# Four value projections of the next pair moved from the end of a part into its middle, and two GpSimd additions tied to later events

## The reference

```
x = LN(x + attention0(x))          # 16 heads of 64, full softmax, output projection + bo
x = LN(x + routed_ffn(x))          # scores against 8 clusters and 64 tiles, two argmaxes pick one
                                   # tile a token; its small spline network scales a direction
x = LN(x + attention1(LN(x)))      # linear attention and a 65-wide window attention, gated, + x
x = LN(x + moe(LN(x)))             # causal attention with normalised q, k; then 8 experts of
                                   # 128 -> 512 -> 128, all computed, mixed by a softmax gate
```

## Time and profile before

| what | us |
|---|---|
| runs (3) | 2326.81, 2313.84, 2310.08; median 2313.84 |
| profiled execution | 2315.99, span 2314.2 |
| TensorE busy | 2190.1 (95% of the span) |
| VectorE, ScalarE, GpSimd busy | 1601.9, 1344.2, 849.3 |
| mean granted TensorE clock | 0.984 of full |

### The profile page before, as it was taken

How to read it: one execution, slowest core, us unless ns; L and a number is a source line. 1 busy time by engine, 2 the same in 40 slices (tenths; PEclk the granted TensorE clock), 3 DMA queues, 4 the chain that set the end, 5 groups by cost and what they waited for, 6 DMA issues and landing times.

```text
span 2314.2 us, 44705 instructions
## 1 busy us (share of the span) xinstructions
PE 2190.1 (95%) x16091; PEld 1532.7 (66%) x16091; DVE 1601.9 (69%) x5015; ACT 1344.2 (58%) x3784; POOL 849.3 (37%) x1010
## 2 busy tenths in 40 slices
PE   8999999999999999999999999999999999999897
PEld 6655666856668566776667666686666856667465
DVE  5666686686767867678775778758676686766752
ACT  5336574764657656576556657476564765646542
POOL 3313471055510644117521356114561064510630
PEclk9999999999999999999999999999999999998999
DMA  4000001000010000110001100001001010010101
GB/s 153 28 1 1 1 1 37 20 33 1 1 56 2 33 1 1 55 34 1 1 10 47 33 2 1 26 31 33 1 1 46 11 33 1 2 46 2 33 3 49
DMA packets 24726, 50.48 MB, mean 22 GB/s; under 512 B 3316, under 2 KB 3900, under 8 KB 24252
## 3 DMA queue, kind: packets, MB, share of 16 engines
q1 hardware_dynamic: 24508, 47.63, 6.3%
HBM read 45.52 MB, written 2.10 MB: 21 GB/s over the span
## 4 chain that ended last, share of the span: by engine, by line
PE 74%; DVE 13%; POOL 5%; ACT 4%; issue 4%; DMA 0%; SPq 0%; ACTq 0%; DVEq 0%; POOLq 0%
PE ps L1534 10%; PE ps L1511 10%; PE ps L651 5%; PE ps L668 5%; PE ps L1546 4%; PE ps L875 4%; PE ps L1460 4%; PE ps L602 4%; PE ps L913 4%; PE ps L1443 4%; PE ps L1415 3%; PE ps L1404 3%; PE ps L805 3%; PE ps L786 2%; PE ps L841 2%
## 5 line engine op out<-in xcount | busy, mean ns | idle before, releaser
L1058 POOL TENSOR_TENSOR rstd<-ve,half_neg 128x4 f32<-128x4 f32 (+1 forms) x56 | 66.9, 1194 | 909.9 <-DVE ve L1039 909.9
L1534 PEld LDWEIGHTS ps<-wbuf,QK 128*128 128x128 f32 x2048 | 263.9, 192 | 97.0 <-issue 95.3
L1325 POOL TENSOR_TENSOR E<-E,ri 128x512 f32<-128x512 f32 x240 | 249.2, 1041 | 147.4 <-DVE ri L1113 147.4
L1637 ACT ACTIVATE QK<-ps,cols 128x512 f32<-128x512 f32 x256 | 172.4, 686 | 196.9 <-PE ps L1511 196.6
L1511 PE MATMUL ps<-h2T,wbuf 128*128 128x512 f32 x512 | 271.1, 619 | 3.7 <-ACT QK L1637 3.7
L1766 POOL TENSOR_TENSOR work<-work,ri 128x128 f32<-128x128 f32 x480 | 231.2, 507 | 117.4 <-DVE ri L1686 116.6
L1534 PE MATMUL ps<-wbuf,QK 128*128 128x128 f32 x2048 | 271.6, 276 | 0.0
L936 ACT ACTIVATE E<-ps,nm 128x256 f32<-128x256 f32 x480 | 225.0, 482 | 73.8 <-DVE nm L1106 73.5
L1759 POOL TENSOR_TENSOR rn<-ss,half_neg 128x8 f32<-128x8 f32 x120 | 195.9, 1638 | 156.6 <-DVE ss L1662 153.5
L1597 ACT ACTIVATE work<-ps,nm 128x128 f32<-128x128 f32 x480 | 202.6, 444 | 64.0 <-DVE nm L1678 63.5
L1106 DVE TENSOR_REDUCE nm<-ps 128x2 f32<-128x512 f32 x256 | 169.8, 681 | 29.3 <-PE ps L651 28.1
(11 more groups left out here) (279 smaller groups left out, 4563.0 us busy)
## 6 DMA issues: line engine op xcount, KB each, us to landing
wbuf<-in_w SPq DMA_DIRECT2D x128, 256.0 KB, 3.2
xT<-in_xT SPq DMA_DIRECT2D x8, 256.0 KB, 3.4
xr<-in_xr SPq DMA_DIRECT2D x8, 256.0 KB, 3.9
bias_t<-in_bias_t SPq DMA_DIRECT2D x1, 2048.0 KB
out_y<-xn SPq DMA_DIRECT2D x8, 256.0 KB, 2.1
wqkv<-in_wqkv SPq DMA_DIRECT2D x1, 1536.0 KB
wo<-in_wo SPq DMA_DIRECT2D x2, 512.0 KB, 7.6
rows<-in_rows SPq DMA_DIRECT2D x1, 531.0 KB, 6.4
```

The lines of the kernel that those rows point to most:

```text
L1325: nc.gpsimd.tensor_tensor(L.E[:, g % 4, :, :], L.E[:, g % 4, :, :], L.ri[:, g, :].unsqueeze(2).broadcast_to((P, NT, S)), ALU.mult)\
L1534: last = nc.tensor.matmul(bank2[2 + x % 2][:, t * P:(t + 1) * P], hid[:, x % 2, c, t * P:(t + 1) * P], w2[:, x % WB, c, :], start=(c == 0) ...
```

## The change

- A new buffer `V_ahead` takes the values of the next pair's first sequence. The four value projections leave the ahead work in parts 1 to 6 (`ahead_pe` runs 8 steps there, 12 only in part 0). They stand in `second_pe` behind the output projections, where the 6 matmuls on constants were, and rotate through two banks, each waiting for ScalarE's copy of the one two before. Part 7 and part 8 keep their matmuls on constants.
- The first-sequence heads read `V_ahead`, so they no longer touch `ETw`.
- L1334 waits for `x3_ready` (the layer norm's last write) in place of `dve1`; L1343 waits for `hotT_ready` (the one-hot choice of tiles, copied) in place of `x1_ready`.
- To make room, the small tensors of the routed network (`ec`, `el`, `fx`, `gates`, ...) move into the spare region of `GQ`, and `vlin1` shrinks to 129 columns a tile.
- All order tables are written anew.

```diff
--- before.py
+++ after.py
@@ the order tables (12 of them, each changed; the tail of one shown) @@
 ("both", "tensor"):
...
-        "111110111010011010011111011011000001000000000000000101010000000020000002000202002200222222",
+        "111111111010010111110100111011101100000000100000000110000001000020000200000000020020002222",
...
+        V_ahead = sb("V_ahead", [P, NT, NH * DH])
...
-        ec = sb("ec", [P, TT * 8])
-        el = sb("el", [P, TT * 8])
-        gates = sb("gates", [P, TT, 8])
...
+        ec, el, fx = part(TT * 8), part(TT * 8), part(TT * 8)
+        gates = part(TT * 8).rearrange("p (t n) -> p t n", t=TT)
+        hot_c = part(TT * 8).rearrange("p (t n) -> p t n", t=TT)
+        hot_l = part(TT * 8).rearrange("p (t n) -> p t n", t=TT)
+        sel = part(TT * TPC).rearrange("p (t n) -> p t n", t=TT)
+        picked = part(TT * 8 * 3).rearrange("p (n a) -> p n a", a=3)
+        vlin1 = sb("vlin1", [P, TT, D + 1])
         kv = sb("kv", [P, NP, D + 1])
...
             pre_proj pre_copied
-        """.split(), (12, 12, 0, 0)))
+        """.split(), (12, 8, 0, 0)))
+        COUNT.update(dict.fromkeys("""
+            v_ahead v_ahead_copied
+        """.split(), (0, 4, 0, 0)))
...
+        first_ahead = first_a._replace(V=V_ahead)
...
                             pe.wait_ge(s["pre_copied"], upto("pre_copied"))
+                            pe.wait_ge(s["v_ahead_copied"], upto("v_ahead_copied"))
                             pe.wait_ge(s["dve1"], upto("dve1"))
...
         def first_pe(pe, both):
             if both:
-                yield from first_heads_pe(pe, first_a, 0, 0, None)
+                yield from first_heads_pe(pe, first_ahead, 0, 0, None)
                 yield from first_heads_pe(pe, first_a, 1, 1, 0)
...
             if both:
                 pool.wait_ge(s["x_next"], upto("x_next"))
-                pool.wait_ge(s["dve1"], upto("dve1"))
+                pool.wait_ge(s["x3_ready"], upto("x3_ready"))
             nc.gpsimd.tensor_tensor(xb[:, :, :], xr[:, :, :], row_t("bo0"), ALU.add).then_inc(s["xb_ready"], 1)
...
-            pool.wait_ge(s["x1_ready"], upto("x1_ready", 1))
+            pool.wait_ge(s["hotT_ready"], upto("hotT_ready", 1))
             nc.gpsimd.tensor_tensor(xb[:, :, :], x1[:, :, :], row_t("beta"), ALU.add).then_inc(s["x1b_ready"], 1)
...
         def ahead_pe(pe, p):
 
-            for u in range(12 if p < PARTS - 2 else 0):
+            for u in range(0 if p >= PARTS - 2 else 8 if p else 12):
                 yield
                 if u == 0:
                     pe.wait_ge(s["x_next"], upto("x_next", 32))
...
         def ahead_act(act, p):
 
-            for u in range(12 if p < PARTS - 2 else 0):
+            for u in range(0 if p >= PARTS - 2 else 8 if p else 12):
                 yield
                 act.wait_ge(s["pre_proj"], upto("pre_proj", u + 1))
                 if u == 0:
                     act.wait_ge(s["w_sc"], upto("w_sc", 8 * NP))
                     act.wait_ge(s["w_av"], upto("w_av", 8 * NP))
-                nc.scalar.activation(first_to(first_a, u), first_from(bank2[u % 3], u), ACT.Copy)\
+                nc.scalar.activation(first_to(first_ahead, u), first_from(bank2[u % 3], u), ACT.Copy)\
                     .then_inc(s["pre_copied"], 1)
...
-        def second_pe(pe, both):
+        def second_pe(pe, p, both):
...
-            yield
-            spare_work(pe, bank2[1], 6 if both else 18)
+            for u in range(4 if both else 0):
+                yield
+                if p < PARTS - 2:
+                    if u == 0:
+                        pe.wait_ge(s["x_next"], upto("x_next", 32))
+                    if u >= 2:
+                        pe.wait_ge(s["v_ahead_copied"], upto("v_ahead_copied", u - 1))
+                    first_proj(pe, bank2[1 + 2 * (u % 2)], 0, 8 + u).then_inc(s["v_ahead"], 1)
+            yield
+            if kind(p) == 1:
+                pe.wait_ge(s["v_ahead_copied"], upto("v_ahead_copied", 4))
+            else:
+                spare_work(pe, bank2[1], 6 if both else 18)
             yield
             pe.wait_ge(s["o2_ready"], upto("o2_ready", 1))
...
-        def second_act(act, both):
+        def second_act(act, p, both):
...
+            for u in range(4 if both else 0):
+                yield
+                if p < PARTS - 2:
+                    act.wait_ge(s["v_ahead"], upto("v_ahead", u + 1))
+                    if u == 0:
+                        act.wait_ge(s["av1"], upto("av1", 8))
+                    nc.scalar.activation(first_to(first_ahead, 8 + u), first_from(bank2[1 + 2 * (u % 2)], 8 + u), ACT.Copy)\
+                        .then_inc(s["v_ahead_copied"], 1)
             yield
```

More of the change, by code:

```diff
@@ L61 @@
     ("both", "vector"):
[L62 to L66, removed]
+        "001010111011010101110110110011011101011011111101011011100111110110110110111010100010101101100011"
@@ L67 @@
+        "110101101100010011101100011101010000110001101011010111111100111110111111110111111111111111101111"
+        "011111111011110011000011001110001001110101001001101100001101010100111001000100111010010001011010"
+        "001000111000100110000110100001111101111001010000000100000000100000000000000010010000000000000000"
+        "1000010001001110100010100110000010100001100010000010010101011001111110101001100000010010000010",
     ("last", "vector"):
-        "000000000010000111101001011110110001101001110110111111110111011101011010110000111011000010011010"
@@ L77 @@
-        "100010101001011010101100010110100111011001011111111111111111010111111111111111110111001111110011"
-        "111110111010011010011111011011000001000000000000000101010000000020000002000202002200222222",
+        "100110101111110010110101101101101110101101101011001110010111100110100111010110101011010010101111"
+        "001100111011101100111110110111001101110110110111110110101101001110001010101001100101101010110110"
+        "100010101001101010101100010111001101011111010101111111111111111101011111111111111111011101001011"
@@ L91 @@
+        "022222",
     ("last", "scalar"):
-        "000000100010101110100111011001111110100011010110011100000111101001111000011100001111001001101000"
-        "11101010011100101001010000000000000000000000000000000000000",
+        "000001000011001101100111011001111110001100111111100000001111000011110000111100001111000011110000"
+        "11110000111100001111000000000000000000000000000000000000000",
     ("first", "gpsimd"):
@@ L100 @@
     ("both", "sync"):
-        "1111110111",
+        "1011111111",
 }
@@ L357, in setup_pool_consts @@
         def setup_pool_consts(pool):
-            for n, (ap, value) in enumerate(((half_neg[:, :], -0.5), (vlin1[:, :, 1, :], 1.0), (gel[COMP:COMP + 1, :], 1.0),
+            for n, (ap, value) in enumerate(((half_neg[:, :], -0.5), (vlin1[:, :, D], 1.0), (gel[COMP:COMP + 1, :], 1.0),
                                              (VW[:, :, :, :, WD], 1.0), (causal[:, :], 0.0))):
@@ L414, in whole_net @@
         names = """
-            x_next
+            x_next v_ahead v_ahead_copied
             y1_ready
@@ L949, in first_act @@
             if both:
-                yield from first_heads_act(act, first_a, 0, 0, None)
+                yield from first_heads_act(act, first_ahead, 0, 0, None)
                 yield from first_heads_act(act, first_a, 1, 1, 0)
@@ L1135, in first_dve @@
             if both:
-                yield from first_heads_dve(dve, first_a, 0, 0, None)
+                yield from first_heads_dve(dve, first_ahead, 0, 0, None)
                 yield from first_heads_dve(dve, first_a, 1, 1, 0)
@@ L1815, in _ @@
                     if first and second:
-                        merged(order(p, "tensor"), first_pe(pe, True), second_pe(pe, True), ahead_pe(pe, p))
+                        merged(order(p, "tensor"), first_pe(pe, True), second_pe(pe, p, True), ahead_pe(pe, p))
                     elif first:
@@ L1819, in _ @@
                     else:
-                        merged(order(p, "tensor"), second_pe(pe, False), second_heads_pe(pe, second_b, 1, 0))
+                        merged(order(p, "tensor"), second_pe(pe, p, False), second_heads_pe(pe, second_b, 1, 0))
             @block.scalar
@@ L1827, in _ @@
                     if first and second:
-                        merged(order(p, "scalar"), first_act(act, True), second_act(act, True), ahead_act(act, p))
+                        merged(order(p, "scalar"), first_act(act, True), second_act(act, p, True), ahead_act(act, p))
                     elif first:
@@ L1831, in _ @@
                     else:
-                        merged(order(p, "scalar"), second_act(act, False), second_heads_act(act, second_b, 1, 0))
+                        merged(order(p, "scalar"), second_act(act, p, False), second_heads_act(act, second_b, 1, 0))
             @block.gpsimd
```

40 lines of the change are left out of this document (16 added, 24 removed).

## The result

The changed kernel takes 2330.08 us (median of 18 runs, 2322.94 to 2348.07), the kernel before 2313.77 on the same chip: ratio 1.0064, 95% interval 1.0049 to 1.0079. So it is slower by about 16 us, 0.7%. That is within 1%, as I gave the most chance to, but 4 us above the end of my range and 16 from the forecast.

What follows compares the result with a forecast made beforehand. TensorE, 95% busy, was taken as the bound. The terms -6.5 - 0.9 + 7.2 - 2.4 + 2.5 summed to -0.1 us, so 2314 us against the median of 2313.84; range 2298 to 2326 us.

Steps and rivals of the forecast that it cites:

- The additions on GpSimd: Both hand-overs: later additions shorten the xn scalings by 0.93 us; -6.5 us at the end, -0.9 in the middle (part 7).
- The value projections in the middle: Middle hand-over, parts 1 to 6: fT comes 2.3 us late, delaying the experts 1.2 us a part, +7.2 us.
- The gate: End hand-over, parts 1 to 6: first half's gate matmuls one place earlier save 0.4 us each, -2.4 us.
- The clock: Behind the end hand-over: the longer gap brings the low clock at 5.5 of seven places, +2.5 us.
- The attention stretch at zero: Attention stretch: same work in a new order, taken as 0, with -1.5 to +1.5 us a part.
- an order that adds 3 us a part: A way to be slower by more than about 1%, beside several rivals at once; chance 0.05.
- Part 0 and part 8: Ordered anew with the same work; taken as 0 together with the attention stretch.
- TensorE doesn't wait at the transposes of the choice of tiles: Rival that it does wait there: late fT makes the routed chain the bound, +6.6 us, 2320 us; chance 0.15.
- no addition collides: Rival that the moved additions meet VectorE's next reductions or routed chain, losing 7.4 us, 2321 us; chance 0.08.
- the faster rival: Attention stretch: new order closes a quarter of its 6.3 us of waits, seven times, 11 us, 2303 us; chance 0.17.
- The clock's rival: Clock falls at every end hand-over, +5 us, with ScalarE's waits in the middle a second place, 2317 us; chance 0.15.

Runs made afterwards that it cites:

- waits_only: The kernel before with only GpSimd's two later waits (x3_ready, hotT_ready), order and value projections as before: 2298.3 us, ratio 0.9926.
- router_before_wait: Changed kernel, x1 transposes after two of the moved projections, fT copied before the third value copy, router matmuls before TensorE's wait for the last copy: 2319.1 us.
- after_again: The changed kernel run and profiled once more, unchanged: 2327.3 us, ratio 1.0050 to the kernel before.
- filled_end_gap: The change with the order of before, plus nine matmuls on constants in the end hand-over before TensorE's wait for the norm: 2312.4 us, ratio 0.9983.
- waits_filled: The kernel before with GpSimd's two later waits, plus matmuls on constants in three waits of the middle hand-over: 2293.9 us, ratio 0.9922.
- changed_filled_gap: The changed kernel with nine matmuls on constants in the end hand-over before TensorE's wait for the norm: 2324.8 us, ratio 1.0044.
- all_but_order: The changed kernel with the order of before: moved value projections, V_ahead and later additions kept, other instructions where they stood: 2332.3 us, ratio 1.0086.
- new_attention_order: The change with nine constant matmuls at the end hand-over and the new order only up to the output projections, order of before after: 2327.7 us, ratio 1.0051.

## Why the prediction was wrong, step by step

- **The additions on GpSimd: right.** 0.94 us at each hand-over against 0.93. By the rule of the Trainium skill, page "SBUF — State Buffer", section "SBUF: two separate sides", that the second of the two stands still until the first has ended, the estimate was 1.20; the runs stay with the row. What I wrote only in passing was the dearer half: with the value projections in the middle its gain there is lost. Against waits_only the move costs 128.49 - 125.45 = 3.0 us a part.
- **The value projections in the middle: right in the main and nearly in size.** From the output projections to the experts' first L1549 (L1534 before) it is 25.35 us against 23.94 (part 2 of both profiles, at full clock), +1.41 a part; predicted +1.2. The late `fT`, on which the prediction put all of it, makes about three quarters (router_before_wait); a quarter is the length of the projections in TensorE's own queue, which it left out.
- **The gate: right.** From L888 to `rstd` 489.31 - 479.38 = 9.93 us against 10.37, -0.44; predicted -0.4.
- **The clock: the size too small, the place wrong.** I priced the end hand-over alone, +2.5 us, with 5.5 falls of 7. The runs show four or none there. That the clock falls in the middle as well stood in the trace of the kernel before: of its seven falls in the six periods four are in the middle hand-over, at 365, 918, 1471 and 1747 us, and I looked only at the end.

```profile
918.00:921.00 3.00, 3.00 (x5) 1.02 (x4) 2.71 (x12) 2.56 (x5) 0.00 (x0) 0.50 0.00 0
```

What the clock cost in the six periods is 1659.7 - 6 x 275.55 = 6.4 us before and 1675.2 - 6 x 277.09 = 12.7 us changed: +6.3. A fall is not worth the same everywhere: 1.65 us behind the end hand-over, about 2 in the attention stretch (for 6.8 us at the low clock); in the middle the first 1.3 us of it are hidden by the wait for ScalarE's table load, so 3.4 us at the low clock cost 0.3 there, and 6.8 us cost 1.8.
- **The attention stretch at zero: this step failed.** "The same work" was true (137.46 us both times) and no ground for a zero, because this stretch is one in which four engines hand each other small pieces, and idle time lies wherever the order leaves a group uncovered. It measured +1.49 us in each of seven parts, 10.4 us. My bounds of 1.5 a part held it, but I turned them into a rival for the faster side only; the slower one was in no rival, only in a chance of 0.05 for an order that adds 3 us a part, and so not in the range. Alone it would have ended at 2324 us, inside the range; with 3.8 us more for the clock and 1.3 more for the move it ends outside.
- **Part 0 and part 8.** No term, and between the profiles of before and after_again they differ by +0.4 and -1.1 us, apart from the stretch at the low clock that some executions have.

In the terms of the prediction: -6.5 - 0.9 + 8.5 - 2.6 + 10.4 + 6.3 = +15.2 us, against 2327.34 - 2311.94 = 15.4 measured beside after_again. So close a match is partly luck. The clock's term counts the six periods only, and the two profiled executions lie just 10.1 us apart (spans 2324.3 and 2314.2): outside the six periods the changed one is 5.4 us shorter, 3.5 of them beside the experts of part 7, where it has 13.7 in place of 20.5 us at the low clock.

Of the rivals, two did not come true: TensorE doesn't wait at the transposes of the choice of tiles, and no addition collides. The attention stretch went the other way than the faster rival had it. The clock's rival was near in size (+5 against +6.3) and right in its second place, the middle, and wrong in the fall at every end hand-over.

The Trainium skill, page "TensorE: Matmul & The Clock Gate", section "HAM oscillation — how this bites in real kernels", has waits between bursts of matmuls bring the clock down again and again. filled_end_gap and waits_filled agree: 58 and 24 us of low time went with matmuls that cost next to nothing. changed_filled_gap shows the limit: in that kernel filling the one long gap took away 7 of 48 us.

Open: what brings the clock down where in the new order. Short waits stand before two of the three places, but before the fall at the gate TensorE was busy 3.88 of 4 us with small matmuls, so waits alone are not the whole of it; falls move from execution to execution, and each kernel has one or two profiles. That the attention side could be had at 148.2 us with the value projections away from it wasn't tried.

## What to carry to other kernels

Work that lies in the shadow of a wait is free where it is; moved to where the engine is busy it costs its length, and it leaves a gap that can cost the clock as well. Filling such gaps with matmuls on constants won back 20 us where the move had opened a long one (all_but_order to filled_end_gap, which is then no faster than the kernel before), and some 5 us of six periods where the waits were short. An order table that is made anew is a change of its own: price it from both sides, and try it apart from the edit that it came with; the one edit of this change that needed no new order, two waits of GpSimd, is worth about 16 us alone, and with the middle hand-over filled 20.

## What the runs showed of the hardware

- In part 0 the clock can stay at 1.2 GHz for 41 us while TensorE is busy 39.22 of 40 us (395 small matmuls), and the same matmuls run through at 2.4 GHz in another execution of the same kernel. new_attention_order's profile, at 2338.4 us, shows it too. It costs about 12 us: the `rstd` that ends part 0 comes at 210.43 us and, in after_again, at 198.49. What brings it about is open.
- With nine matmuls of 0.24 us at the end hand-over, with no result that anyone reads, the falls just behind them are gone, and so are falls some 160 us further on, in the middle hand-over: 65 to 7 us of low time in one execution of each kernel, and 20 us between the medians.
